# Computing v = x·wv by seven block products instead of eight, from batch 1 on, in a transformer block on one Trainium2 core

## The chip, the core and the metric

The kernel runs on one core of one Trainium2 chip. A core has five engines that run their own instruction streams and meet only at semaphores: TensorE (PE in the profile; its weight loads are listed as PEld), VectorE (DVE), ScalarE (ACT), GpSimd (POOL) and SyncE (SP), which here issues every DMA. TensorE writes its results into eight banks of PSUM, each 128 partitions by 512 float32 columns. The metric is device time in microseconds for one execution; lower is better.

## What is computed

The reference is one transformer block over 16 batches of 512 tokens of width 256 (8 heads of 128): a layer norm without scale, causal attention with rotary positions, and a feed-forward net with weights of +1 and -1, both added to the input.

```
xn = layernorm(x)                                # x: (16, 512, 256)
q, k, v = xn@wq, xn@wk, xn@wv                    # (b, h, 512, 128) each
q, k = rope(q), rope(k)
p = softmax(q@k.T / 128 - 1e30*(i < j))          # causal
attn = (p@v) @ wo
h = 2*relu(s0 * [xn, -xn]@(+-k0))                # 1024 wide
h = 2*relu(s1 * h@(+-k1))                        # 1024 x 1024
out = x + attn + s2 * h@(+-k2)
```

The change touches `xn@wv` in batches 1 to 15, how the partial sums of the 1024 x 1024 layer are held, and the order of everything.

## The kernel before, in words

**Precision by halves.** Each float32 operand is split into two float16 numbers, HI and LO (the rest), and a product is three matmuls: HI·HI, HI·LO, LO·HI. ACT makes a HI by a copy with a cast (`v_hi`, `o_hi`, `qk_hi`, `xp_hi`, `split_w_hi`), DVE or POOL makes the LO by a subtraction (`v_lo`, `o_lo`, `split_w_lo` on DVE, `qk_lo`, `xp_lo`, `h0t_lo` on POOL). The weights of +1 and -1 are exact in fp8, so products with them need two matmuls.

**x.** For batch b, SP loads x (`load_x`), DVE makes its statistics (`stats`), POOL normalises it (`normalise`) into the place in `XT` where its transpose will stand, ACT and POOL split it into `XP` (`xp_hi`, `xp_lo`), and SP's `turn_x` transposes XP by DMA into `XT`, from which all of the batch's first matmuls read. XT has two places, one for even and one for odd batches.

**v.** `v_proj(b, grp, t)` makes 128 tokens (tile t) of 4 heads (group grp) of v: 6 matmuls of 128 x 512, stationary operand from XT, moving operand 512 columns of wv. A batch has 8 of them, so 48 matmuls of 512 columns.

**Attention.** Per head and batch: `qk` (6 matmuls of 512 columns for q, 6 for k), rotation (`swap` on ACT, `crossed` on POOL, `straight` and `rotate` on DVE), `scores` into three banks, softmax (`row_max` on DVE, `exponent` on ACT, `inverse` on DVE, `p_hi`, `p_lo`), `turn_p` on SP (two DMA transposes of P), `values`, `o_hi`, `o_lo`, and for each half batch `project` with wo and `add_attn`, `send`.

**Feed-forward.** `layer0` makes h0 transposed. The 1024 x 1024 layer is made in blocks of 512 by a seven-product scheme already: DVE makes differences of h0's quarters (`difference`), POOL made the weights' sums once (`combine`), and `product(j, p, ...)` is product p of 7 for column half j, 16 matmuls of 256 columns. Products 1 and 6 build running sums in a bank; where a sum is needed twice, ACT copies the bank (`copy_sum`, three times for each j); product 5 is kept in SBUF (`keep_p5`) and added by DVE (`add_p5`). Then `h1_hi`, `h1_lo`, and `layer2`.

**Order.** Nothing is scheduled at run time. Each engine's stream is written out in the code: `sync_program`, `gpsimd_program`, `scalar_program`, `vector_program`, `tensor_program`. A call stands behind the `wait_ge` lines that it needs. Batches 4 to 14 are a loop (`for b in range(4, 15)`; on TensorE to 13), in which the names of the banks go by a table, `ROTATION`. An engine takes its instructions strictly in this order, so whatever stands behind a waiting instruction waits too. The first 60 us or so also hold the loading, scaling and splitting of the weights: `largest`, `power_of_two`, `powers`, `split_w_hi` and `split_w_lo` (12 of each: 4 for q, 4 for k, 2 for v, 2 for wo), `convert_k1`, `weight_block`, `combine`.

The helper `chain` records most of the simple matmuls, which is why q, k, v, layer 0 and wo all show as L238 in the profile. L699 is `product`, L683 `values`, L666 `scores`, L710 `layer2`.

## Time and profile before

| | |
|---|---|
| time, median of 3 runs | 1728.72 us (1728.67 to 1729.3) |
| the profiled execution: time, span | 1728.13 us, 1726.3 us |
| granted TensorE clock, mean | 0.999 |
| PE busy | 1713.5 us (99%), 12752 matmuls |
| PEld, DVE, ACT, POOL busy | 1202.2, 1386.2, 1467.6, 890.4 us (70%, 80%, 85%, 52%) |
| DMA | 134.08 MB moved, queues 40.1% of 16 engines' span |

Busy time is the time in which at least one instruction of the engine was under way. Matmuls are pipelined: the page's "mean ns of one" is from a matmul's start to the end of its drain (379 ns for 512 columns), while matmuls in a row start closer together than that; what a matmul costs is therefore read from long runs, a stretch of so many us divided by its count. The line "idle before, releaser" names the engine whose event ended most of the idle time before a group. An "issue" time is the engine's own sequencer. Windows give an engine's busy time in a stretch; in the steady part one batch is one period. A few records of matmuls can be missing from a trace, so counts are taken from the program.

### The profile page before, as it was taken

To read this page: it belongs to the slowest core of one execution; us is meant where nothing else is said; L and a number is where in the kernel's file an instruction comes from. 1 tells how busy PE (TensorE), PEld (TensorE's weight loads), DVE (VectorE), ACT (ScalarE), POOL (GpSimd) and SP (SyncE) were. 2 spreads that over 40 slices of the span, in tenths; PEclk is the share of its full clock that TensorE was granted. 3 is DMA by queue.
4 is the path that set the end of the run, shared out by engine and by line. 5 is a ranking of instruction groups with operands and counts; after the bars stand their busy time and mean duration, and the time that the engine had idled before them with its cause. 6 is when DMAs were issued, how large, how long until landed. Compare 5 with 4: busy or idle time off the path is not lost.

```text
span 1726.3 us, 34270 instructions
## 1 busy us (share of the span) xinstructions
PE 1713.5 (99%) x12752; PEld 1202.2 (70%) x12752; DVE 1386.2 (80%) x3374; ACT 1467.6 (85%) x3229; POOL 890.4 (52%) x696
## 2 busy tenths in 40 slices
PE   8999999999999999999999999999999999999999
PEld 4567667677676776767667676676767767677677
DVE  8997887887878878688787877878788787886875
ACT  7898897888979889798897988979789797897984
POOL 7654655354654635556354563555635556354531
PEclk9999999999999999999999999999999999999999
DMA  5234434343434433444434343344433534353343
GB/s 177 56 72 85 93 60 93 68 90 64 76 81 65 98 60 71 86 72 83 68 62 86 74 81 68 68 85 70 92 56 82 79 61 93 58 94 71 62 81 68
DMA packets 454838, 134.08 MB, mean 78 GB/s; under 512 B 434704, under 2 KB 453648, under 8 KB 454672
## 3 DMA queue, kind: packets, MB, share of 16 engines
q1 hardware_dynamic: 454672, 131.90, 40.1%
q8 instruction: 100, 1.64, 0.4%
q14 instruction: 66, 0.54, 0.1%
HBM read 14.94 MB, written 8.39 MB: 14 GB/s over the span
## 4 chain that ended last, share of the span: by engine, by line
PE 95%; ACT 2%; DVE 2%; DMA 1%; SPq 0%; issue 0%; POOL 0%; DVEq 0%; ACTq 0%
PE bank L238 44%; PE bank L699 21%; PE bank L683 12%; PE bank L666 12%; PE bank L710 6%; DMA v<-in_wk 1%; ACT bank L427 1%; DVE pt L514 0%; ACT ph L431 0%; DMA xnat<-in_x 0%; DVE hb L549 0%; DVE ph L585 0%; SPq L282 0%; DVE wq L537 0%; ACT tb L409 0%
## 5 line engine op out<-in xcount | busy, mean ns | idle before, releaser
L351 POOL TENSOR_TENSOR tb<-tb,sin 128x512 f32<-128x512 f32 x256 | 324.7, 1273 | 445.4 <-ACT tb L410 442.7
L354 POOL TENSOR_TENSOR qk<-tb,qk 128x512 f16<-128x512 f32 x256 | 295.7, 1160 | 284.3 <-ACT qk L413 284.1
L699 PE MATMUL bank<-hb,wa 128*128 128x256 f16 x3360 | 391.3, 273 | 0.2 <-DVE ph L585 0.2
L699 PEld LDWEIGHTS bank<-hb,wa 128*128 128x128 fp8e5 x3360 | 327.3, 98 | 53.7 <-DVE ph L585 0.4
L427 ACT ACTIVATE bank<-bank,nm,sc 128x512 f32<-128x512 f32 (+3 forms) x512 | 301.3, 591 | 2.6
L585 DVE SCALAR_TENSOR_TENSOR ph<-bank,rk,ph 128x512 f16<-128x512 f32 (+3 forms) x512 | 254.1, 545 | 23.0 <-ACT ph L431 21.3
L575 DVE CUSTOM_DVE_ANT_0 bank<-bank,mask 128x512 f32<-128x512 f32 (+3 forms) x512 | 238.5, 518 | 20.4 <-PE bank L666 20.1
L557 DVE TENSOR_TENSOR bank<-bank,cos 128x512 f32<-128x512 f32 x256 | 176.7, 697 | 87.3 <-ACT tb L410 87.1
L683 PEld LDWEIGHTS bank<-pt,v 128*128 128x128 f16 x2304 | 203.7, 98 | 41.5 <-DMA pt<-ph 0.8
L431 ACT ACTIVATE ph<-bank,rk 128x512 f16<-128x512 f32 (+3 forms) x512 | 230.1, 541 | 2.4 <-DVE rk L582 1.4
L683 PE MATMUL bank<-pt,v 128*128 128x256 f16 (+1 forms) x2304 | 231.1, 255 | 0.0
L666 PE MATMUL bank<-qk 128*128 128x512 f16 (+3 forms) x1536 | 229.6, 299 | 0.8 <-POOL qk L354 0.7
L413 ACT ACTIVATE qk<-tb 128x512 f16<-128x512 f32 x256 | 159.5, 635 | 48.9 <-PE bank L666 27.1
L666 PEld LDWEIGHTS bank<-qk 128*128 128x128 f16 x1536 | 133.6, 98 | 93.1 <-POOL qk L354 1.9
L561 DVE TENSOR_TENSOR tb<-bank,tb 128x512 f32<-128x512 f32 x256 | 175.0, 685 | 23.4 <-POOL tb L351 22.6
L238 PE MATMUL bank<-xT,wq 128*128 128x512 f16 x768 | 187.6, 381 | 3.2 <-DVE wq L537 3.2
L409 ACT ACTIVATE tb<-bank 64x512 f32<-64x512 f32 x256 | 151.9, 593 | 42.0 <-PE bank L238 33.8
L238 PE MATMUL bank<-wv,xT 128*128 128x512 f16 x768 | 185.2, 379 | 0.3 <-DVE ph L585 0.3
L238 PE MATMUL bank<-xT,wk 128*128 128x512 f16 x768 | 184.4, 379 | 0.0
L238 PE MATMUL bank<-wo,o 128*128 128x256 f16 x1536 | 172.9, 273 | 0.0
L238 PEld LDWEIGHTS bank<-wo,o 128*128 128x128 f16 x1536 | 150.1, 98 | 20.9
L358 POOL TENSOR_TENSOR hb<-rt,hb 128x1024 f16<-128x1024 f32 x60 | 127.8, 2130 | 55.7 <-ACT hb L443 55.7
(113 smaller groups left out, 2343.9 us busy)
## 6 DMA issues: line engine op xcount, KB each, us to landing
out<-xnat SPq DMA_DIRECT2D x32, 256.0 KB, 2.2
xnat<-in_x SPq DMA_DIRECT2D x15, 512.0 KB, 3.8
pt<-ph SPq DMA_TRANSPOSE x256, 4.3
o<-in_k SPq DMA_DIRECT2D x1, 1024.0 KB, 7.5
v<-in_wq SPq DMA_DIRECT2D x1, 1024.0 KB, 9.5
v<-in_wk SPq DMA_DIRECT2D x1, 1024.0 KB, 11.3
ph<-in_wv SPq DMA_DIRECT2D x1, 1024.0 KB, 13.5
o<-in_wo SPq DMA_DIRECT2D x1, 1024.0 KB, 10.9
```

Source lines behind the costliest of these rows:

```text
L238: m = pe.matmul(ps[:, cols[0]:cols[1]], l, r, start=start and n == 0, stop=signal is not None and n == last)
L351: pool.tensor_tensor(tb, tb, SIN[:], ALU.mult).then_inc(s_crossed, 1)
L354: pool.tensor_tensor(QK[:, g % 2, 2 * w + 1, :], TB[:, (2 * g + w) % TRING, :], QK[:, g % 2, 2 * w, :], ALU.subtract).then_inc(s_qk_lo, 1)
L427: act.activation(p, p, ACT.Exp, bias=NM[:, g % 4, i:i + 1], scale=SC[:, 0:1], accum_out=SM[:, g % 4, i:i + 1]).then_inc(s_exp, 1)
L431: act.activation(part(g, i, HI), tile_of(ps, i), ACT.Copy, scale=RK[:, g % 4, i:i + 1]).then_inc(s_P_hi, 1)
L557: dve.tensor_tensor(ps[:, :], ps[:, :], COS[:], ALU.mult).then_inc(s_straight, 1)
L561: dve.tensor_tensor(tb, ps[:, :], tb, ALU.add).then_inc(s_rot, 1)
L575: dve.tensor_tensor_reduce(out=s, in0=s, in1=MASK[:, 512 - WIDTH[i]:512], scale=1.0, scalar=-3.0e38, op0=ALU.add, op1=ALU.max, accum_out=M ...
L585: dve.scalar_tensor_tensor(part(g, i, LO), tile_of(ps, i), RK[:, g % 4, i:i + 1], part(g, i, HI), ALU.mult, ALU.subtract).then_inc(s_P_lo, 1)
L666: mm = pe.matmul(ps[:, col:col + w], l, m, start=i == tiles[0] and n == 0, stop=end)
L683: mm = pe.matmul(ps[:, 128 * i0:128 * i1], l, m, start=n == 1, stop=n == 18)
L699: mm = pe.matmul(ps[:, 256 * u:256 * u + 256], WA[:, w, k, (2 * j + u) * 128:(2 * j + u) * 128 + 128], HB[:, h, s, k, :], start=first and ...
```

## The change

Four things change.

1. **v by seven products.** In batches 1 to 15 the product x·wv is cut into 2 x 2 blocks (two token tiles by 128 of x's columns; 128 of wv's rows by 256 of its columns) and made by seven block products with running sums. `v_product(b, grp, p)` is 6 matmuls of 256 columns; a batch has 2 x 7. x's four sums are made by POOL from the normalised x (`x_sums`, 4 instructions), split (`tp_hi` on ACT, `tp_lo` on POOL) and transposed by a second DMA transpose (`turn_t`) into a new buffer `XS`, one for all batches. The running sums are copied by ACT (`copy_sum`, twice for each group), product 5 is kept in SBUF (`keep_v5`) and added by DVE (`add_v5`, twice for each group). The weights' four sums are made once by POOL (`v_weight_sum`), and eight blocks of wv are split instead of two larger ones. `v_hi` and `v_lo` write the same number of tiles as before.
2. **Batch 0** keeps eight products (`v_first`), with 12 matmuls of 256 columns for a tile instead of 6 of 512.
3. **Layer 1 with two copies** of running sums for each j instead of three; for one of the two sums that need product 5, DVE's addition writes into another bank (`add_p5_to`).
4. **All orders** are new, on all engines, the first batches and the last one included.

To make room, small buffers are merged (`RS` into `VE`, `RI` into `NM`, `RK` into `MX`, the identity and the scales into PT's start). XN of every batch now goes through XS: POOL's `normalise(b+1)` writes there and waits for batch b's last v product.

```diff
+V_PRODUCTS = {1: (0, 0, 0, 0), 2: (1, 0, 0, 1), 3: (6, 0, 2, 1), 4: (2, 1, 0, 1), 5: (3, 1, 0, 0), 6: (4, 1, 2, 1),
+              7: (5, 1, 2, 0)}
...
-        W = {n: sb("w" + n, [128, 2, 2048], F16) for n in "qkvo"}
+        W = {n: sb("w" + n, [128, 2, 2048], F16) for n in "qko"}
+        WV = sb("wv", [128, 7, 2, 512], F16)
...
+        XS = sb("xs", [128, 2, 4, 2, 128], F16)
...
+        def turn_t(sp, b):
+            sp.dma_start_transpose(XS[:].rearrange("p s t c n -> p (s t c) n"),
+                                   XP.rearrange("p s t m -> p (s t m)")).then_inc(s_xTT, 16)
...
+        def x_sums(pool, b):
...
+            pool.tensor_tensor(t1, b12, b11, ALU.subtract).then_inc(s_t1, 1)
+            pool.tensor_tensor(t3, b22, b12, ALU.subtract)
+            pool.wait_ge(s_t1, b)
+            pool.tensor_tensor(t2, b22, t1, ALU.subtract).then_inc(s_t2, 1)
+            pool.wait_ge(s_t2, b)
+            pool.tensor_tensor(t4, b21, t2, ALU.subtract).then_inc(s_tt, 1)
...
+        def keep_v5(act, ps):
+            act.activation(V5, ps[:, :], ACT.Copy).then_inc(s_v5, 1)
...
+        def add_v5(dve, ps, dst):
+            dve.tensor_tensor(dst[:, :], ps[:, :], V5, ALU.add).then_inc(s_vadd, 1)
...
+        def add_p5_to(dve, ps, dst):
+            dve.tensor_tensor(dst[:, :], ps[:, :], S5, ALU.add).then_inc(s_add, 1)
...
-        def v_proj(pe, b, grp, t, ps):
-            operands = []
-            for c in range(2):
-                operands += three(lambda s: XT[:, b % 2, s, t, c, :],
-                                  lambda s: W["v"][:, s, c * 1024 + grp * 512:c * 1024 + grp * 512 + 512])
-            chain(pe, ps, (0, 512), operands, s_v)
...
+        def v_product(pe, b, grp, p, ps):
+            w, buffer, t, c = V_PRODUCTS[p]
+            src = XS if buffer else XT[:, b % 2]
+            for u in range(2):
+                operands = three(lambda s: src[:, s, t + u, c, :], lambda s: WV[:, w, s, grp * 256:grp * 256 + 256])
+                for n, (l, r) in enumerate(operands):
+                    end = u == 1 and n == 2
+                    mm = pe.matmul(ps[:, 256 * u:256 * u + 256], l, r, start=p in (1, 5) and u == n == 0, stop=end,
+                                   skip_group_check=True)
...
         ROTATION = [
-            [0, 5, 1, 3, 4, 2, 6, 7],
+            [2, 0, 1, 7, 4, 5, 3, 6],
...
```

**TensorE, middle of a batch.** In rows before, inside batch 7, the v products are eight lots of 6 matmuls of 512 columns (`bank<-wv,xT 128x512`), and the first matmul that needs the next batch's x (the wait for s_xT) stands behind all products of layer 1 (L699) but one:

```order
L699 MATMUL bank1<-hb,wa 128x256 x16
L238 MATMUL bank0<-wv,xT 128x512 [waits s_h1]
L238 MATMUL bank0<-wv,xT 128x512 x5
L683 MATMUL bank3<-pt,v 128x256 [waits s_P_lo,s_pt1]
...
L238 MATMUL bank6<-xT,wq 128x512 [waits s_xT,s_P_lo]
L238 MATMUL bank6<-xT,wq 128x512 x5
```

In rows of the changed kernel, in the same batch (its names of lines: L803 `product`, L276 `chain`, L754 `scores`, L792 `v_product`), the wait for s_xT stands in the middle of layer 1, and the v products that wait for the transposed sums (s_xTT) and for copies (s_copy) follow, in lots of 6 matmuls of 256 columns:

```order
L803 MATMUL bank5<-hb,wa 128x256 x16
L276 MATMUL bank6<-xT,wq 128x512 [waits s_xT,s_o]
L276 MATMUL bank6<-xT,wq 128x512 x5
L276 MATMUL bank4<-xT,wq 128x512 [waits s_h1]
...
L792 MATMUL bank1<-wv,xT 128x256 [waits s_copy]
L792 MATMUL bank1<-wv,xT 128x256 x5
L792 MATMUL bank4<-wv,xs 128x256 [waits s_xTT]
L792 MATMUL bank4<-wv,xs 128x256 x5
```

What moved: the next batch's x is now needed with four products of layer 1 still to come, where it was needed with one to come, and the lots of v are narrower and wait for more.

**SP, one batch.** Before, x's transpose (`xT<-rt`) is followed at once by the transposes of P:

```order
L252 DMA xnat<-in_x 128x4x256 [waits s_out01,s_out00]
L282 DMA_TRANSPOSE pt<-ph 128x16x128 [waits s_PV,s_P_lo]
L282 DMA_TRANSPOSE pt<-ph 128x8x128
L282 DMA_TRANSPOSE pt<-ph 128x16x128 [waits s_PV]
L282 DMA_TRANSPOSE pt<-ph 128x8x128
L276 DMA_TRANSPOSE xT<-rt 128x16x128 [waits s_xp]
L282 DMA_TRANSPOSE pt<-ph 128x16x128 [waits s_PV,s_P_lo]
```

In the changed kernel a second transpose stands between them, for the sums (`xs<-rt`), with a wait of its own:

```order
L290 DMA xnat<-in_x 128x4x256 [waits s_out01,s_out00]
L324 DMA_TRANSPOSE pt<-ph 128x16x128 [waits s_PV]
L324 DMA_TRANSPOSE pt<-ph 128x8x128
L324 DMA_TRANSPOSE pt<-ph 128x16x128 [waits s_PV,s_P_lo]
L324 DMA_TRANSPOSE pt<-ph 128x8x128
L314 DMA_TRANSPOSE xT<-rt 128x16x128 [waits s_xp]
L318 DMA_TRANSPOSE xs<-rt 128x16x128 [waits s_tp]
L324 DMA_TRANSPOSE pt<-ph 128x16x128 [waits s_PV,s_P_lo]
```

What moved: the next P's transposes now also wait for s_tp.

**TensorE, the start.** Before, layer 0 of batch 0 (`xT,w0`) begins when the first quarter of its weights is signed, and one lot waits for h0's bank; layer 1 (`hb`) begins on the first of h0:

```order
L238 MATMUL bank2<-xT,w0 128x512 [waits s_xT0,s_W0]
L238 MATMUL bank2<-xT,w0 128x512
L238 MATMUL bank2<-xT,w0 128x512 [waits s_xT0]
...
L238 MATMUL bank2<-xT,w0 128x512 [waits s_h0]
L238 MATMUL bank2<-xT,w0 128x512 x3
L238 MATMUL bank3<-hb 128x512 [waits s_h0,s_W1]
...
L238 MATMUL bank4<-dg,pt 128x2
```

In the changed kernel the last lot of layer 0 stands behind the scale's power (`128x2`, waits s_pow), and layer 1's third step waits for the last of h0:

```order
L276 MATMUL bank1<-pt 128x128 [waits s_largest]
L276 MATMUL bank4<-pt 128x2 [waits s_ones,s_pow]
L276 MATMUL bank3<-xT,w0 128x512 x4
L276 MATMUL bank2<-hb 128x512 [waits s_W1]
L276 MATMUL bank2<-hb 128x512 x3
L276 MATMUL bank2<-hb 128x512 [waits s_W1]
L276 MATMUL bank2<-hb 128x512
L276 MATMUL bank2<-hb 128x512 [waits s_h0]
```

On ACT the step that makes that last of h0 from bank 3 (`hb<-bank3`) stands behind five copies of layer 1's weights (`wa`, L443) and one split of wq (L465); before, all eight such steps stood ahead of them:

```order
L468 ACTIVATE hb<-bank6 128x512
L443 ACTIVATE wa<-rt 128x1024 [waits s_W1a]
L443 ACTIVATE wa<-hb 128x1024 [waits s_W1]
L443 ACTIVATE wa<-hb 128x1024 [waits s_W1a]
L443 ACTIVATE wa<-hb 128x1024
L443 ACTIVATE wa<-rt 128x1024
L465 ACTIVATE wq<-v,kn 128x2x256 [waits s_w_in_q,s_KN]
L468 ACTIVATE hb<-bank3 128x512 [waits s_l0]
```

What moved: one eighth of h0 is made later, and layer 1 of batch 0 waits for it.

## Rows read from the trace of the kernel before

**Rows 1.** Page: busy time of the engines.
```profile
PE 1713.5 (99%) x12752; PEld 1202.2 (70%) x12752; DVE 1386.2 (80%) x3374; ACT 1467.6 (85%) x3229; POOL 890.4 (52%) x696
```
**Rows 2.** Windows, one period: length, busy PE, PEld, DVE, ACT, POOL, clock, DMA.
```profile
460.35:566.46 106.11, 106.11 (x802) 75.27 (x800) 85.17 (x210) 91.00 (x202) 54.73 (x43) 1.00 0.43 75
```
**Rows 3.** Chain of waits in time: start, length, what, count.
```profile
294.05 5.24 PE bank L699 x48
430.93 3.88 PE bank L238 x18
1674.50 1.63 PE bank L666 x12
1717.37 1.65 PE bank L683 x18
```
**Rows 4.** Groups by line and form: busy us, mean ns of one, idle before.
```profile
L238 PEld LDWEIGHTS bank<-wv,xT 128*128 128x128 f16 x768 | 74.4, 98 | 70.1 <-DVE ph L585 0.8
L446 ACT ACTIVATE bank<-bank 128x512 f32<-128x512 f32 x90 | 53.5, 594 | 22.4 <-PE bank L699 21.4 <-DVE h L605 1.0
L405 ACT ACTIVATE rt<-xT 128x1024 f16<-128x1024 f32 x15 | 15.9, 1063 | 0.0
L602 DVE TENSOR_TENSOR bank<-bank,rt 128x512 f32<-128x512 f32 x60 | 41.7, 695 | 12.9 <-PE bank L699 10.7 <-ACT bank L446 1.0
L351 POOL TENSOR_TENSOR tb<-tb,sin 128x512 f32<-128x512 f32 x256 | 324.7, 1273 | 445.4 <-ACT tb L410 442.7
L347 POOL TENSOR_TENSOR rt<-xT,rt 128x1024 f16<-128x1024 f32 x15 | 31.9, 2128 | 2.9 <-ACT rt L405 2.9
L537 DVE SCALAR_TENSOR_TENSOR wv<-ph,kn,wv 128x1024 f16<-128x1024 f32 x2 | 2.7, 1368 | 0.0
```
**Rows 5.** Timeline of PE at the start: start, length, instruction, idle before.
```profile
31.38 1.89 PE L238 MATMUL bank<-xT,wq 128*128 128x512 f16 x4 [3.20 <-DVE wq L537]
```
**Rows 6.** Timeline of ACT at the start.
```profile
22.02 3.00 ACT L378 ACTIVATE wa<-hb 128x1024 fp8e5<-128x1024 f16 x3
26.28 1.38 ACT L396 ACTIVATE wq<-v,kn 128x512 f16<-128x512 f32 x2
```
**Rows 7.** Timeline of DVE: the last of the reductions, and splits of weights.
```profile
25.80 2.27 DVE L514 TENSOR_REDUCE pt<-o 128x1 f32<-128x2048 f32 x1
62.27 1.32 DVE L537 SCALAR_TENSOR_TENSOR wo<-o,kn,wo 128x1024 f16<-128x1024 f32 x1
68.45 3.15 DVE L537 SCALAR_TENSOR_TENSOR wo<-o,kn,wo 128x1024 f16<-128x1024 f32 x1
```
**Rows 8.** Timeline of POOL beside the last of these.
```profile
68.39 2.12 POOL L347 TENSOR_TENSOR rt<-xT,rt 128x1024 f16<-128x1024 f32 x1 [2.92 <-ACT rt L405]
```
**Rows 9.** Windows at the start, columns as in rows 2.
```profile
20.00:40.00 20.00, 16.04 (x68) 6.97 (x67) 19.79 (x30) 17.53 (x26) 18.42 (x10) 0.91 0.20 64
40.00:60.00 20.00, 19.68 (x102) 9.58 (x101) 19.59 (x49) 17.22 (x32) 17.49 (x21) 1.00 0.01 2
```
**Rows 10.** Timeline of one batch: PE's step behind `project`, x's transpose, its first use.
```profile
1011.82 1.46 PE L238 MATMUL bank<-xT,wk 128*128 128x512 f16 x6
1034.71 1.92 SPq L276 DMA_TRANSPOSE xT<-rt  x1
1056.87 1.46 PE L238 MATMUL bank<-xT,wq 128*128 128x512 f16 x6
```
**Rows 11.** Line L282 (`turn_p`), all of them: from issue to landing.
```profile
DMA to landing us min/median/max: 3.1/4.3/6.1
```
**Rows 12.** Line L276 (`turn_x`), all of them: from issue to landing.
```profile
DMA to landing us min/median/max: 4.2/4.2/4.6
```
**Rows 13.** Timeline of SP: the last pair of `turn_p`.
```profile
1709.79 3.72 SPq L282 DMA_TRANSPOSE pt<-ph  x2
```
**Rows 14.** Windows behind it, columns as in rows 2 (last: DMA's share, GB/s).
```profile
1711.00:1712.00 1.00, 1.00 (x12) 0.90 (x10) 0.00 (x0) 0.00 (x0) 0.00 (x0) 1.00 1.08 209
1714.00:1715.00 1.00, 1.00 (x11) 0.90 (x10) 0.46 (x1) 0.51 (x1) 0.00 (x0) 1.00 0.80 148
```

More of the change, by code:

```diff
@@ L809, in sync_program @@
             turn_p(sp, 11)
-            sp.wait_ge(s_xp, 2)
-            turn_x(sp, 2)
+            sp.wait_ge(s_tp, 2)
+            turn_t(sp, 2)
             sp.wait_ge(s_P_lo, 52)
@@ new lines, in tensor_program @@
+            pe.wait_ge(s_rot, 19)
+            values(pe, 7, BANK[7])
+            v_product(pe, 1, 1, 7, BANK[1])
+            pe.wait_ge(s_rot, 20)
+            product(pe, 0, 1, range(8), BANK[4], first=True)
+            pe.wait_ge(s_vadd, 4)
+            v_product(pe, 1, 1, 4, BANK[1])
+            pe.wait_ge(s_qk_lo, 18)
+            scores(pe, 8, 0, BANK[6])
+            pe.wait_ge(s_rot, 21)
+            scores(pe, 8, 1, BANK[0])
+            pe.wait_ge(s_vp, 15)
+            scores(pe, 8, 2, BANK[3])
@@ new lines, in tensor_program @@
+            pe.wait_ge(s_P_lo, 80)
+            values(pe, 16, BANK[1])
+            pe.wait_ge(s_h1, 9)
+            product(pe, 1, 1, range(8), BANK[3], first=True)
+            pe.wait_ge(s_copy, 14)
+            product(pe, 0, 7, range(8), BANK[4])
+            product(pe, 0, 3, range(8), BANK[2])
+            pe.wait_ge(s_pt[1], 288)
+            pe.wait_ge(s_rot, 44)
+            values(pe, 17, BANK[7])
+            pe.wait_ge(s_qk_lo, 43)
+            pe.wait_ge(s_rot, 45)
+            scores(pe, 20, 0, BANK[0])
@@ L6065, in tensor_program @@
+            scores(pe, 114, 2, BANK[5])
             pe.wait_ge(s_sum, 27)
@@ new lines, in tensor_program @@
+            values(pe, 112, BANK[1])
+            pe.wait_ge(s_h1, 105)
+            product(pe, 1, 1, range(8), BANK[3], first=True)
+            pe.wait_ge(s_copy, 110)
+            product(pe, 0, 7, range(8), BANK[4])
+            product(pe, 0, 3, range(8), BANK[2])
+            pe.wait_ge(s_pt[1], 1824)
+            pe.wait_ge(s_rot, 236)
+            values(pe, 113, BANK[7])
+            pe.wait_ge(s_qk_lo, 235)
+            pe.wait_ge(s_rot, 237)
+            scores(pe, 116, 0, BANK[0])
```

8750 lines of the change are left out of this document (4813 added, 3937 removed), and 26 rows, old and new, of the table ROTATION.

## The prediction

> **What bounds the kernel now.** The first view is the page's line of busy times: TensorE is busy 1713.5 of 1726.3 us, ScalarE 85%, VectorE 80%, GpSimd 52% [rows 1]. A busy share says nothing yet, so the second view is a window of exactly one batch: in 106.11 us TensorE is busy 106.11, ScalarE 91.00, VectorE 85.17, GpSimd 54.73, at a granted clock of 1.00 [rows 2]. There is no idle time on TensorE to take away in the middle; only fewer or shorter matmuls help, and whatever makes TensorE wait costs in full. The third view, the chain of waits, gives what a matmul costs in a row: 48 matmuls of 256 columns take 5.24 us, 109.2 ns each; 18 of 512 columns take 3.88 us, 215.6 ns each [rows 3]. The fourth is the start, where TensorE does wait: 3.20 us for the first weights of q [rows 5], while VectorE is busy 39.4 us of the 40 from 20 to 60 us [rows 9]. So two places matter: a batch's matmuls, fifteen times, and the start, once, where VectorE is the full engine.
>
> **The sum of the matmuls.** Per batch v takes 8 x 6 = 48 matmuls of 512 columns: 48 x 215.6 ns = 10.35 us. By seven products it takes 2 x 7 x 6 = 84 of 256 columns: 84 x 109.2 ns = 9.17 us [rows 3]. The gain is 1.18 us a batch, 17.7 us over batches 1 to 15. It is a little under one part in eight of v, since 2 x 109.2 - 215.6 = 2.8 ns of each matmul don't shrink with its width. Batch 0's eight products become 96 of 256 columns: 96 x 109.2 = 10.48 us, 0.13 us more. No other matmul is added or taken away, so TensorE's work falls by 17.6 us. All the rest of the change can only take from this.
>
> **Weight loads.** Each matmul here loads its own stationary operand, 98 ns [rows 4], and a product's 109.2 ns leaves 11 ns beside it. Products of layer 1 already run in this form, one load for each 256 columns, and their pace is the one used above; so I charge the loads nothing. The Trainium skill (TensorE: Matmul & The Clock Gate, section Back-to-back issue gap) says that in a real stream of loads and matmuls the pace is set by both, and gives 131 ns for 512 columns and 81 ns for 128. By it, with an estimate of 98 ns for 256 columns on the line between the page's two, v would go from 6.3 to 8.2 us a batch, and the change would cost 28 us where the rows give 17.6 back. The trace here contradicts the pace of 131 ns.
>
> **Work added to the other engines, per batch.** ScalarE: two more copies in all (four for v, two fewer for layer 1) and two `keep_v5`, each like L446's 594 ns, and `tp_hi`, like `xp_hi`'s 1063 ns: 3.4 us, so 94.4 us of a period of 104.9 us, 90%. VectorE: four `add_v5` like L602's 695 ns: 2.8 us, so 88.0 us, 84%. GpSimd: `tp_lo` like L347's 2128 ns, and four additions of 256 elements; these have no row, and lie between 532 ns (a quarter of L347's) and 1273 ns (L351, twice their size) [rows 4]. I take 0.85 us, on the line through the two: 5.5 us, so 60 us, 57%. All three stay under TensorE, so by amount they cost nothing. What they can cost is lateness: an engine at 90% in a fixed order serves a request late more often. The nearest rows are two periods of before without any wait at 91.00 of 106.11; the bounds are nothing and, say, two copies' length a batch. I take nothing, and leave the rest to the rivals.
>
> **Copies.** A copy of a running sum now stands close behind its product: `v_product(b,1,1)` is followed by one head's scores, 1.63 us [rows 3], and then `v_product(b,1,6)` waits for the copy, 0.594 us [rows 4]. About 1 us is left over. Between product 6 and product 3, which also waits for a copy, stand two products of 0.66 us; 0.7 us is left. In before the closest such pair had a q or k product and one of layer 1 between, 3 us. If ScalarE is in the middle of something else, each of these places waits for up to one instruction of its queue.
>
> **x's transpose.** Counted from the end of `project(b-1, 1)`, TensorE reached the first use of the next batch's x after 45.05 us (1056.87 - 1011.82), and the transpose was issued after 22.9 us, so with 4.2 us to land it had some 18 us to spare [rows 10, 12]. Now five q or k lots (1.295 us each, a third of 3.88), nine products of layer 1 (1.747 each, a third of 5.24), two `values` (1.65) and one head's scores (1.63) stand between [rows 3]: 6.5 + 15.7 + 3.3 + 1.6 = 27.1 us. SP's queue puts the transpose behind two pairs of `turn_p`, and the second pair waits for `values(8b+1)`, which ends after four of these lots, six products and two `values`: 19.0 us. A pair takes SP 3.72 us [rows 13] and its transfers last to 5.0 us behind its start (from 1709.79 to 1714.80, the last window being busy for 0.80 us) [rows 14]. x's own 2048 columns, 0.52 MB at the 209 GB/s of that view, take 2.5 us behind them. So xT lands at 19.0 + 5.0 + 2.5 = 26.5 us against a need at 27.1. It is just in time, and I charge nothing; the upper bound comes from the slowest landing of `turn_p`, 6.1 against a median of 4.3 us [rows 11]: 1.2 us of waiting a batch, or 1.8 if my count of the margin is off by its 0.6. Behind `turn_x` now stands `turn_t`, which waits for `tp_lo`, and behind that the next P's transposes. The sums are through at about 35 us (`xp_lo` at 20.5, four additions, the rotations between, `tp_hi`, `tp_lo`), and the `values` that needs that P comes at 47 us, so this wait is covered.
>
> **The start.** Now one eighth of h0 is made late: on ScalarE it stands behind five copies of about 1.0 us (3.00 us for three) and a split of q, which puts it at 28.1 us where before q's splits began at 26.28 [rows 6]. VectorE's reduction of wo ends at 28.1 anyway [rows 7], so h0 is complete at 28.8. Then come 10 matmuls of one lot of layer 1 and 16 of the next, 26 x 215.6 ns = 5.6 us, and q's first lot starts at 34.4 us instead of 31.38 [rows 5]. That is 3.0 us. Before, that lot began at the low clock of 1.2 GHz (four matmuls in 1.89 us, 0.91 granted over the window [rows 5, 9]), after 3.20 us of waiting; if it begins at 2.4 GHz now, 1.3 us come back. I take 2.4 us of 1.7 to 3.0. Further, VectorE splits eight lots of 512 elements for v where it split two of 1024 in 2.7 us [rows 4]. A lot of 1024 took 1.32 us, and 3.15 us when GpSimd ran a two-input operation beside it [rows 7, 8]: so 2.6 to 9.9 us more. VectorE has no room before 60 us, but four of the eight can come later, and are ordered so. I take 1.6 us, near the low end, of 0 to 9.9. The start costs 4.0 us together.
>
> **The end.** The last head's `values` began at 1717.37 and its P had landed at 1714.80: 2.6 us to spare [rows 3, 14]. Between its scores and that `values` stood 60 matmuls with wo, both halves of `layer2` and one `values` (6.6 + 7.0 + 1.6 = 15.2 us at 109.2 ns a matmul of 256 columns); now one `values` more and one half of `layer2` less, 13.3 us. 0.7 us are left: nothing.
>
> **The sum.** 1728.13 us of the profiled execution (its span of 1726.3 us and 1.8 around it) - 17.6 + 4.0 = 1714.5 us; the median of the runs lies 0.6 us above it: 1715.1. I forecast 1715 us.
>
> **The rivals.**
> 1. Copies served late. For: ScalarE at 90%, and 0.7 to 1 us of room at two places a batch. Against: nothing in the steady part of before waited at 86%. One copy's length, 0.6 us, a batch at 14 batches: + 8.3, 1723 us.
> 2. VectorE bounds the start. For: 39.4 of 40 us busy. Against: half the new splits are put off. The upper end of 9.9 instead of 1.6 us: 1723 us.
> 3. xT comes late (the other side). Place: the first q lot of the next batch, batches 2 to 15. For: a margin of 0.6 us by my count, two pairs of transposes ahead of it on one queue, landings up to 6.1 us [rows 11]. Against: x's own landings were all within 4.2 to 4.6 [rows 12]. With 1.3 us a batch, 14 x 1.3 = + 18.2: 1733 us. It decides from 1.0 us a batch on, where the gain is gone.
> 4. The start is no worse than before: TensorE's order makes up the late eighth of h0. 1711 us.
> 5. Weight loads are not hidden: 98 + 107 ns for each narrow matmul, 84 x 205 ns = 17.2 us a batch, + 6.9 x 15: some 1830 us. Against: L699's pace. The Trainium skill's page on TensorE, cited above, speaks for this one, with a smaller price.
>
> **Chances.** Forecast (1712 to 1719 us) 0.57; rival 1, 0.15; rival 2, 0.08; rival 3, 0.11; rival 4, 0.08; rival 5, 0.01. Range: below, rival 4 and 2 us of its own uncertainty, 1709; above, to the middle of rival 3 between no wait and 1.3 us, 1729. Within 0.2% (3.5 us, what a measurement of this kernel can tell from no change) is 1725.3 to 1732.2. Rivals 1, 2 and 4 and the forecast are faster but for their upper tails; rival 3 is split between same and slower. Faster 0.82, same 0.09, slower 0.09.
>
> **What would show it.** In a window of one batch: a period of 104.9 us, TensorE busy all of it, ScalarE 94.4, VectorE 88.0, GpSimd 60. Narrow v matmuls at 109 ns in the chain. TensorE's waits: none by name in the middle; a wait on the DMA of xT repeated 14 times would be rival 3, one on ScalarE's copy in a bank rival 1. At the start the first matmul with wq at 34.4 us and TensorE's idle time up to 60 us some 3 to 4 us more than before. The prediction is wrong if the period is over 106 us, or if TensorE is idle over 25 us in all.

## The result, and the profile after

| | before | after |
|---|---|---|
| time, median (4 runs each) | 1728.7 us (1728.59 to 1729.3) | 1745.33 us (1743.47 to 1747.16) |
| profiled execution: time, span | 1728.13, 1726.3 us | 1747.16, 1745.4 us |

The change makes the kernel slower: ratio 1.0095, 95% interval 1.0078 to 1.0113. The forecast was 1715 us with a range of 1709 to 1729; the result lies outside it, 30 us above the forecast, and on the other side of the kernel before. The page's line of busy times, which answers to [rows 1]:

```profile
PE 1706.3 (98%) x13340; PEld 1258.5 (72%) x13340; DVE 1425.0 (82%) x3440; ACT 1514.8 (87%) x3310; POOL 968.1 (55%) x775
```

TensorE is busy 7.2 us less, in a span 19.1 us longer: its idle time is 39.1 us where it was 12.8. Who ended it is in the view of waits (engine, line, who was waited for, us in total, times, longest):

```profile
PE bank L771 <- DMA pt<-ph: 7.8, 10, 1.4
PE bank L276 <- DMA xT<-rt: 5.8, 11, 1.2
PE bank L276 <- DVE pt L606: 4.8, 1, 4.8
PE bank L276 <- ACT w L435: 3.0, 1, 3.0
PE bank L754 <- DVE tb L639: 2.6, 1, 2.6
PE bank L754 <- POOL qk L419: 2.4, 3, 1.6
...
PE bank L276 <- DVE tb L639: 1.6, 1, 1.6
```

The first two are of the steady part, about once a batch each (one of the ten waits for P is at the very end), the next two of the start, and the others shown of batches 0 to 2. Windows of the changed kernel say how much each stretch holds (columns as in rows 2), and the last two rows show the start, whose clock was 1.00 and 0.91:

```profile
60.00:300.00 240.00, 229.40 (x1740) 162.32 (x1739) 207.89 (x514) 218.03 (x488) 140.65 (x116) 1.00 0.41 78
300.00:1670.00 1370.00, 1357.48 (x10788) 1013.51 (x10786) 1121.33 (x2736) 1206.49 (x2650) 767.67 (x606) 1.00 0.44 80
...
0.00:20.00 20.00, 13.89 (x54) 9.57 (x55) 12.58 (x28) 10.02 (x14) 11.39 (x19) 0.75 0.93 320
20.00:40.00 20.00, 15.24 (x60) 6.64 (x58) 17.84 (x20) 16.54 (x23) 18.23 (x11) 0.82 0.19 61
```

The same two long windows of the kernel before, which were not shown above:

```profile
60.00:300.00 240.00, 239.09 (x1736) 161.79 (x1734) 199.55 (x489) 213.77 (x483) 134.49 (x104) 1.00 0.43 82
300.00:1670.00 1370.00, 1369.95 (x10317) 969.95 (x10316) 1100.53 (x2704) 1177.30 (x2606) 700.04 (x537) 1.00 0.41 75
```

So from 300 us on TensorE waits 12.5 us where it waited 0.05, between 60 and 300 us 10.6 where it waited 0.9, at the end once for 1.4, and up to 60 us 2.3 us more: 25.9 us together. Two things come on top, both estimates from rows. In front of a wait the last matmul's drain counts as busy, while in a row of matmuls the next one starts before it is over (273 - 109 ns, or 379 - 216): 0.165 us for each of 26 more waits (36 against 10), 4.3 us. And the low clock at the start, below, costs some 4 us more than before. Against that stands what the seven products save, 16.4 us: 1.10 us a batch (below) in 15 batches, less the 0.13 us of batch 0. 25.9 + 4.3 + 4 - 16.4 = 17.8 us, of the span's 19.1.

**One batch.** A window over eleven batches, from one start of `project` to the same eleven batches later:

```profile
378.07:1546.74 1168.67, 1158.43 (x9199) 864.53 (x9197) 957.83 (x2343) 1031.67 (x2267) 655.22 (x517) 1.00 0.44 80
```

That is a period of 106.24 us, where 104.9 was forecast and 106.11 was before, with 0.93 us idle in each. In batch 6 the transposes on SyncE, first the row of both pairs of P's, then the second pair by itself, x's and the sums' transposes, and, from the chain, the time from x's issue to its landing. Then TensorE's lot behind `project`, and its first lot with the next batch's x:

```profile
726.27 10.64 SPq L324 DMA_TRANSPOSE pt<-ph  x4
733.20 3.71 SPq L324 DMA_TRANSPOSE pt<-ph  x2
736.96 3.29 SPq L314 DMA_TRANSPOSE xT<-rt  x1
749.95 1.97 SPq L318 DMA_TRANSPOSE xs<-rt  x1
736.96 5.42 DMA xT<-rt
```
```profile
714.01 1.46 PE L276 MATMUL bank<-xT,wq 128*128 128x512 f16 x6
742.51 2.75 PE L276 MATMUL bank<-xT,wq 128*128 128x512 f16 x12 [1.22 <-DMA xT<-rt]
```

And one batch on, `values` of the fifth head (h = 4), and before it the issue of its P's transpose:

```profile
862.50 1.91 SPq L324 DMA_TRANSPOSE pt<-ph  x1
```
```profile
860.62 3.55 PE L771 MATMUL bank<-pt,v 128*128 128x256 f16 x36
864.00 0.82 PE L792 MATMUL bank<-wv,xT 128*128 128x256 f16 x6
864.66 0.82 PE L792 MATMUL bank<-wv,xs 128*128 128x256 f16 x6
865.31 1.79 PE L754 MATMUL bank<-qk 128*128 128x512 f16 x12
866.94 1.47 PE L792 MATMUL bank<-wv,xs 128*128 128x256 f16 x12
869.72 1.82 PE L771 MATMUL bank<-pt,v 128*128 128x256 f16 x18 [1.31 <-DMA pt<-ph]
```

The row x36 is two heads' `values`, 2 and 3. P has two places (`s_pt[0]` and `s_pt[1]`), so head 4's transpose waits until head 2's `values` has read the first, at 860.62 + 1.65 = 862.27 us; it is issued at 862.50. P itself had been complete since 850.0 us, when VectorE's last `p_lo` of that head ended, so only the place was missing. Between the two `values` stand 5.9 us of matmuls, and from the first issue to the second landing the pair takes 7.2 us here (to 869.68). In the trace of the kernel before, no two `values` that share a place stood closer than 10.5 us (10.6 us in batch 7, from 805.75 to 816.36), and no pair took longer than 7.3 us. The wait for the sums' transpose (xs, issued 855.45) has nothing to do with it.

**The start.** TensorE's rows that answer to [rows 5]:

```profile
14.32 9.15 PE L276 MATMUL bank<-xT,w 128*128 128x512 f16 x28 [3.04 <-ACT w L435]
23.31 0.38 PE L276 MATMUL bank<-pt 128*128 128x128 f32 x2
28.45 0.59 PE L276 MATMUL bank<-pt 128*128 128x2 f32 x2 [4.76 <-DVE pt L606]
28.90 1.87 PE L276 MATMUL bank<-xT,w 128*128 128x512 f16 x4
30.56 4.43 PE L276 MATMUL bank<-hb 128*128 128x512 f16 x12
...
39.15 1.46 PE L276 MATMUL bank<-xT,wq 128*128 128x512 f16 x6
```

Layer 0 begins at 14.32 us (before: 12.02), since its first lot needs the last of four signs of k0. Its 28 matmuls take 9.15 us where 28 x 215.6 ns are 6.0: the granted clock is 1.2 GHz for half of these 20 us (0.75 in the window above), and it had fallen already in the window from 10 to 11 us (0.53), ahead of the wait for the signs. Then TensorE waits 4.76 us for the power of two, which stands on VectorE behind the maximum of wv, and in that wait, between 27 and 28 us, the clock falls a second time (0.56). The first lot with wq comes at 39.15 us, not at 34.4.

### The profile page after: what moved, and what is told of

The parts are those of the page before. It is cut to its first block, busy times and chain, and to the rows that moved or that the text cites. A ratio compares the mean times of both kernels' runs of the same rounds, so it can differ in the third digit from the quotient of the medians.

```text
span 1745.4 us, 35757 instructions
## 1 busy us (share of the span) xinstructions
PE 1706.3 (98%) x13340; PEld 1258.5 (72%) x13340; DVE 1425.0 (82%) x3440; ACT 1514.8 (87%) x3310; POOL 968.1 (55%) x775
## 4 chain that ended last, share of the span: by engine, by line
PE 79%; ACT 6%; DMA 6%; DVE 4%; SPq 3%; issue 1%; POOL 1%; DVEq 0%; ACTq 0%
PE bank L276 32%; PE bank L803 16%; PE bank L771 10%; PE bank L754 9%; PE bank L792 6%; PE bank L814 5%; SPq L324 3%; DMA xT<-rt 3%; DMA pt<-ph 3%; ACT bank L505 2%; DVE ph L670 1%; POOL tb L416 1%; ACT tb L485 1%; ACT tb L484 1%; DVE bank L660 1%
## 5 line engine op out<-in xcount | busy, mean ns | idle before, releaser
L803 PE MATMUL bank<-hb,wa 128*128 128x256 f16 x3360 | 388.2, 273 | 0.0
L803 PEld LDWEIGHTS bank<-hb,wa 128*128 128x128 fp8e5 x3360 | 328.1, 98 | 49.9
L505 ACT ACTIVATE bank<-bank,nm,sc 128x384 f32<-128x384 f32 (+3 forms) x512 | 302.8, 595 | 2.7
L670 DVE SCALAR_TENSOR_TENSOR ph<-bank,mx,ph 128x512 f16<-128x512 f32 (+3 forms) x512 | 254.1, 543 | 12.7 <-ACT ph L509 11.8
L660 DVE CUSTOM_DVE_ANT_0 bank<-bank,mask 128x128 f32<-128x128 f32 (+3 forms) x512 | 238.0, 512 | 2.6 <-PE bank L754 2.0
L509 ACT ACTIVATE ph<-bank,mx 128x512 f16<-128x512 f32 (+3 forms) x512 | 231.0, 537 | 5.3 <-DVE mx L667 3.6
L754 PE MATMUL bank<-qk 128*128 128x512 f16 (+3 forms) x1536 | 230.1, 299 | 5.1 <-DVE tb L639 2.6
L754 PEld LDWEIGHTS bank<-qk 128*128 128x128 f16 x1536 | 132.4, 98 | 91.4 <-POOL qk L419 3.8
L276 PE MATMUL bank<-xT,wq 128*128 128x512 f16 x768 | 184.7, 379 | 7.5 <-DMA xT<-rt 5.8
L276 PE MATMUL bank<-xT,wk 128*128 128x512 f16 x768 | 184.1, 379 | 1.3 <-DVE v L645 0.9
L484 ACT ACTIVATE tb<-bank 64x512 f32<-64x512 f32 x256 | 151.9, 593 | 26.5 <-PE bank L276 20.2
L276 PE MATMUL bank<-wo,o 128*128 128x256 f16 x1536 | 172.9, 273 | 0.0
L276 PEld LDWEIGHTS bank<-wo,o 128*128 128x128 f16 x1536 | 150.3, 98 | 20.3
L485 ACT ACTIVATE tb<-bank 64x512 f32<-64x512 f32 x256 | 150.6, 588 | 3.1
```

What stands on the lines that cost most here:

```text
L276: m = pe.matmul(ps[:, cols[0]:cols[1]], l, r, start=start and n == 0, stop=signal is not None and n == last)
L505: act.activation(p, p, ACT.Exp, bias=NM[:, g % 4, i:i + 1], scale=SC[:, 0:1], accum_out=SM[:, g % 4, i:i + 1]).then_inc(s_exp, 1)
L509: act.activation(part(g, i, HI), tile_of(ps, i), ACT.Copy, scale=RK[:, g % 4, i:i + 1]).then_inc(s_P_hi, 1)
L660: dve.tensor_tensor_reduce(out=s, in0=s, in1=MASK[:, 512 - WIDTH[i]:512], scale=1.0, scalar=-3.0e38, op0=ALU.add, op1=ALU.max, accum_out=M ...
L670: dve.scalar_tensor_tensor(part(g, i, LO), tile_of(ps, i), RK[:, g % 4, i:i + 1], part(g, i, HI), ALU.mult, ALU.subtract).then_inc(s_P_lo, 1)
L754: mm = pe.matmul(ps[:, col:col + w], l, m, start=i == tiles[0] and n == 0, stop=end)
```

## Experiments

Each was timed beside the kernel before on the same chip. Given are the median, the ratio to the kernel before with its 95% interval, and mostly the difference to the changed kernel's 1745.3 us. The kernel before took 1728.6 to 1729.0 us in the different groups of runs, so a difference between runs of two groups carries up to 0.4 us more doubt than its medians show.

### SyncE: x's transpose ahead of the second pair of P's

```diff
+                sp.wait_ge(s_xp, b + 1)
+                turn_x(sp, b + 1)
                 sp.wait_ge(s_P_lo, 32 * b + 16)
                 sp.wait_ge(s_PV, 8 * b + 2)
                 turn_p(sp, 8 * b + 3)
                 sp.wait_ge(s_xp, b + 1)
-                turn_x(sp, b + 1)
```

> SyncE's order alone: from batch 3 on the next batch's x is transposed ahead of the second pair of P's transposes instead of behind it. Theory A (two tight places in one batch, xT at the first q lot and P of the fifth head at its values, that cover for each other: what one lets through the other takes): the 11 waits on xT (5.8 us idle) go, those on P of the fifth head grow; 1742 us, 1740 to 1745. Theory B (the two places are independent): 1745.3 - 7.6 = 1738 us. Theory C (another engine, ScalarE at 90 per cent, sets the period of 106.2 us, and the waits only show it): 1745 us, no change.

Measured: 1738.52 us, 1.0057 (1.0044 to 1.0069), 6.8 us less. No wait on xT is left; those on P hardly change:

```profile
PE bank L771 <- DMA pt<-ph: 7.2, 8, 1.5
```

Theory B's 7.6 us is nearly there; A's 3 us and C's nothing are refuted.

### TensorE: the fifth head's values 2.4 us later

```diff
                 v_product(pe, b + 1, 0, 7, ps[5])
+                pe.wait_ge(s_vp, 8 * b + 9)
+                v_product(pe, b + 1, 0, 3, ps[4])
+                product(pe, 1, 4, range(8), ps[2])
                 pe.wait_ge(s_pt[0], 128 * b + 96)
                 pe.wait_ge(s_vp, 8 * b + 9)
                 values(pe, 8 * b + 4, ps[1])
-                v_product(pe, b + 1, 0, 3, ps[4])
-                product(pe, 1, 4, range(8), ps[2])
```

> TensorE's order alone: the values of each batch's fifth head stand behind the next v product and product 4 of layer 1's second half (2.4 us later) from batch 2 to 13. Theory A: the waits on P of the fifth head go, those on xT grow from 0.2 to 1.2 us a batch; 1742 us, 1739 to 1745. Theory B (independent places): 1745.3 - 5.5 = 1740 us. Theory C: 1745 us.

Measured: 1741.37 us, 1.007 (1.0056 to 1.0083), 4.0 us less. The waits on P fall from 7.8 to 3.1 us and those on xT grow by a tenth:

```profile
PE bank L276 <- DMA xT<-rt: 6.4, 12, 1.3
PE bank L771 <- DMA pt<-ph: 3.1, 4, 1.4
```

### Both

> Both of the two edits before together. Theory A: neither wait is left, the period falls from 106.24 to the 104.9 us of its matmuls over 12 batches, 1745.3 - 15 = 1730 us, 1729 to 1733. Theory B: 1745.3 - 7.6 - 5.5 = 1732 us, so this run alone does not tell A from B, but with the two single ones it does. Theory C: the waits move to ScalarE or VectorE and the time stays over 1740 us.

Measured: 1733.06 us, 1.0023 (1.0013 to 1.0033), 12.3 us less; the two alone make 10.8. The places are nearly independent (B); theory A, that what one lets through the other takes, is wrong. P still makes TensorE wait 3.6 us, at five places. And the period is what the matmuls make of it; a window from one `project` to the next:

```profile
903.71:1008.72 105.01, 105.01 (x839) 78.78 (x837) 86.94 (x213) 93.78 (x208) 59.61 (x47) 1.00 0.44 81
```

TensorE is busy all of 105.01 us, 1.10 us less than the 106.11 of [rows 2]. ScalarE at 93.78, VectorE at 86.94 and GpSimd at 59.61 are where the prediction put them (94.4, 88.0, 60), and none makes TensorE wait. What two reorderings repair is what the new order had broken.

### The price of a product, with the order repaired

The run all_warm, on which this one rests, is the last of the start's kernels below.

```diff
                 operands = three(lambda s: src[:, s, t + u, c, :], ...)
+                if p == 7:
+                    operands = operands + operands
                 for n, (l, r) in enumerate(operands):
-                    end = u == 1 and n == 2
+                    end = u == 1 and n == len(operands) - 1
```

> The kernel of the run all_warm, in which the last of the seven products of v runs its six matmuls twice (v is not the reference's then), so that TensorE has as many narrow matmuls for v as eight products would take: 12 more of 256 columns a batch, 180 in all. Theory A (with the two places repaired TensorE alone bounds the period, and a product left out is worth its matmuls): 180 x 109.2 ns = 19.7 us more, 1747 us, 1746 to 1748. Theory B (ScalarE or VectorE nearly bound the period too): under 16 us more, 1740 to 1743 us.

Measured: 1744.5 us, 1.0094 (1.008 to 1.0107), 17.2 us above all_warm. One batch is 106.33 us, TensorE busy throughout:

```profile
800.62:906.95 106.33, 106.33 (x850) 79.94 (x849) 87.05 (x214) 94.01 (x207) 59.59 (x47) 1.00 0.41 80
```

That is 1.32 us more than the 105.01 us above, for 12 matmuls, 110 ns each, load and all: theory A in every batch, 19.7 us in 15. The total is 2.5 us less than that and lies between the ranges given for A (1746 to 1748 us) and B (1740 to 1743). TensorE is idle 23.1 us in this run and 25.5 in all_warm; the waits for P in batch 14 (0.5 us) and at the very end (1.5 us) are gone.

### The order of k0's signs alone

ScalarE signs, and VectorE subtracts, block 0 first and block 3 last, and TensorE's first lot waits for one instead of four:

```diff
-            pe.wait_ge(s_W0, 4)
+            pe.wait_ge(s_W0, 1)
             pe.wait_ge(s_xT0, 1)
             layer0(pe, 0, 1, 0, BANK[2])
```

> The changed kernel with nothing but the order of the four signs of k0 changed, so that TensorE's first lot of layer 0 needs the first of them and not the last. It begins at 12.3 instead of 14.3 us. Theory A (what bounds the start behind it is VectorE's power of two, 27.3 to 28.4 us, behind its maximum of wv): nothing comes of it, 1745 us, at most 1 us less. Theory B (TensorE's late start and low clock bound the start): 1745.3 - 2 to 3 = 1742.5 to 1743 us.

Measured: 1744.28 us, 1.0088 (1.0074 to 1.0102), 1.0 us less, which theory A allows; a difference of that size is within the spread of both kernels' runs. Layer 0 starts at 12.38 us, 1.9 us sooner, and TensorE then waits longer for the power of two:

```profile
12.38 8.12 PE L276 MATMUL bank<-xT,w 128*128 128x512 f16 x28 [0.69 <-DVE xT L588]
20.34 0.38 PE L276 MATMUL bank<-pt 128*128 128x128 f32 x2
25.78 0.59 PE L276 MATMUL bank<-pt 128*128 128x2 f32 x2 [5.05 <-DVE pt L606]
```

### The start: signs, power of two and the last eighth of h0

Beside the signs, in excerpts:

```diff
             largest_of_all(dve, 0, BANK[1])
-            dve.wait_ge(s_w_in["v"], 16)
-            largest(dve, 2)
+            dve.wait_ge(s_am_max, 1)
+            power_of_two(dve, 0)
...
             h0_first_hi(act, 4, BANK[6])
+            act.wait_ge(s_l0, 8)
+            h0_first_hi(act, 3, BANK[3])
...
+            layer1(pe, 0, range(2, 3), BANK[2])
             pe.wait_ge(s_pow, 1)
             pe.wait_ge(s_ones, 1)
             spread_power(pe, 0, BANK[4])
```

> The start alone: the block of k0 that TensorE's first lot of layer 0 needs is subtracted and signed first instead of last, so TensorE starts at 12.1 instead of 14.3 us; VectorE makes the power of two right behind the maximum of all, and its maximum of wv later; the last eighth of h0 is made ahead of the five copies of layer 1's weights; the small matmuls that spread the power stand behind layer 1's first three steps. Theory A (the start's loss is made there): first wq matmul at 32 to 34 us instead of 39.15, 17 us of half clock shrink to 3 to 7, and the time is 1745.3 - 6 = 1739 us, 1737 to 1741. Theory B (VectorE is the full engine of the start; what TensorE gains before 40 us it waits away at its first scores and between 60 and 140 us): 1743 to 1745 us.

Measured: 1741.96 us, 1.0074 (1.0062 to 1.0087), 3.4 us less, between the ranges of the two theories. The first lot of wq comes at 33.49 us, 5.7 us sooner, after 2.5 us of waiting for wq's split on VectorE. At the low clock (0.91 from 20 to 40 us) its six matmuls take 2.23 us instead of 1.46, and 3.9 us of the 5.7 are left from 60 us on. All waits behind stand where they stood, 3.9 us earlier and as long as before (2.63, 0.40, 1.05, 0.93 us): what is gained here is not waited away there.

### Everything so far together

With two small edits more: `v_product(1, 0, 6)` behind `qk(7, 0)`, and the last head's P on VectorE ahead of `add_ffn(15, 0)`.

> The start's edits and the two of the steady part together, and two small ones: in batch 1 the v product that waited for ScalarE's copy of a running sum (1.02 us at 124 us) stands behind one q lot more, and at the end VectorE makes the last head's P ahead of an addition of the feed-forward net that stood before it. Theory A (the losses stand at separate places and add up): 1733.1 - 3.4 (start) - 1.2 (copy) - 0.7 (end) = 1728 us, 1726 to 1730. Theory B (something gained at the start is waited away later, since VectorE and ScalarE are full up to 140 us): 1730 to 1733 us.

Measured: 1728.54 us, 1.0001 (0.9992 to 1.001): theory A. The losses were at separate places and add up; the kernel is where it was before the change. The two small edits moved waits more than they removed them: the wait for the copy in batch 1 (1.02 us) is gone, but 0.92 us is waited one lot later, and P at the end still comes 1.5 us late.

### Dummy products at the start

```diff
             turn_first(pe, 0, BANK[0], BANK[1])
+            zeros(pe, 1, BANK[7])
...
-            zeros(pe, 2, BANK[7])
+            zeros(pe, 5, BANK[7])
```

> The kernel of the run before with five more dummy products of zeros in TensorE's first 12 us (one behind each of the first two transposes of x, three more in front of layer 0), which fill its idle time there. Theory A (the idle time before 12 us is why the granted clock falls to 1.2 GHz at about 10 us): the clock stays at 2.4 GHz up to the wait for wq, layer 0's seven lots take 6 instead of 8.6 us, TensorE then waits for other engines for part of it; 1 to 2 us less than the run before. Theory B (the clock falls there whatever TensorE does, or the time gained is waited away at the first of wq): the same time within 0.5 us, or up to 0.5 us more from the dummy products.

Measured: 1727.27 us, 0.9991 (0.9982 to 1.0000), 1.3 us below the run before: theory A in kind. The granted clock is 1.00 over the first 20 us (0.91 in all_fixed, where layer 0's 28 matmuls took 7.99 us), and 26 matmuls of layer 0 take 5.79 us:

```profile
13.39 5.79 PE L276 MATMUL bank<-xT,w 128*128 128x512 f16 x26 [0.41 <-DVE xT L588]
```

This is the best version that computes the reference. Against the kernel before it is not a difference that can be told from none. The saving is in it all the same: TensorE is busy 1700.0 us, 13.5 less than before, and idle 25.5 us, 12.7 more. Of that idle time 9.6 us more stand between 60 and 300 us, 1.8 us more between 300 and 1670, and 1.5 us at the end.

### VectorE's splits of wv cut short

In the kernel of all_fixed, `split_w_lo` for v makes 64 columns of each group of 256 (GpSimd zeroes the low halves once).

> The kernel of the run before the last with VectorE's eight splits of wv's blocks cut to an eighth of their width and no more (64 of 512 columns; the rest of wv's low halves is zero, so v is less exact): VectorE has some 6 us less work up to 100 us. Theory A (VectorE's added splits bound TensorE between 60 and 240 us): the waits at 65 to 135 us (2.6, 0.4, 0.9, 0.3, 0.6 us) go in the main, 3 to 5 us less than with whole splits. Theory B (these waits come from ScalarE's chain and the order of single instructions): 0 to 1.5 us less.

Two groups of 64 are a quarter of 512, not the eighth that the expectation says: the eight splits take 5.0 us instead of 9.4. Measured: 1727.97 us, 0.9994 (0.9985 to 1.0003), 0.6 us below all_fixed. That is theory B, and not more than the runs' spread. The wait at 64 us is 2.63 us instead of 2.81, and those at 125 to 133 us are as long as they were (0.9, 0.7, 0.3, 0.6). Half of the splits stand in front of the first, all of them in front of the others: with 4.4 us less work on VectorE, its splits are not their cause.

### Single instructions earlier in batches 0 and 1

```diff
             straight(dve, BANK[7])
+            dve.wait_ge(s_crossed, 6)
+            dve.wait_ge(s_straight, 6)
+            rotate(dve, 2, 1, BANK[7])
+            dve.wait_ge(s_x[1], 16)
+            stats(dve, 1)
             dve.wait_ge(s_S, 4)
             row_max(dve, 1, 3, BANK[1])
...
+            rotate(dve, 14, 0, BANK[4])
             dve.wait_ge(s_S, 41)
             row_max(dve, 13, 2, BANK[2])
...
+            qk_hi(act, 14, 0)
             act.wait_ge(s_inv, 13)
             act.wait_ge(s_pt[0], 192)
             p_hi(act, 12, 3, BANK[5])
```

The same calls are taken out further down, and on GpSimd `crossed(2, 1)` stands ahead of `combine(6, 0)`.

> The kernel of the run all_warm with four single instructions moved in batches 0 and 1: VectorE rotates the third head's k ahead of x's statistics and of two row maxima, GpSimd makes its crossed part ahead of a sum of layer 1's weights; VectorE rotates the q of head 14 ahead of a row maximum, and ScalarE makes its high half ahead of four pieces of P. Theory A (the waits of batches 0 to 2 are single instructions too late in a fixed order): the 2.8 us wait at 64 us shrinks to 1.5 or less, those of 1.6 and 1.7 us at 213 and 217 us to 1.5 together; 1727.3 - 2.5 = 1725 us. Theory B (ScalarE and VectorE are full there, so that what is made earlier makes something else later): the sum of the waits between 60 and 240 us stays within 1 us of its 9.5 us, 1727 us.

Measured: 1730.87 us, 1.001 (1.0001 to 1.0019), 3.6 us above all_warm: worse than either theory. Of all_warm, then of this run, TensorE at 64 us:

```profile
63.72 0.50 PE L754 MATMUL bank<-qk 128*128 128x256 f16 x3 [2.81 <-DVE tb L639]
64.62 1.47 PE L276 MATMUL bank<-xT,wk 128*128 128x512 f16 x6 [0.41 <-DVE ph L670]
```
```profile
66.45 2.27 PE L276 MATMUL bank<-xT,wk 128*128 128x512 f16 x6 [3.96 <-DVE ph L670]
```

The wait for the rotation is gone, but the next lot needs P, which VectorE makes later now: 2.81 + 0.41 became 3.96 us in one piece. Behind it six matmuls of 512 columns take 2.27 instead of 1.47 us, at a lower granted clock: in the window of 60 to 80 us it is 0.91, where all_warm has 1.00. The same happens at 223 us (1.58 + 1.65 + 0.85 became 0.44 + 1.54 + 1.93 us, clock 0.91 from 220 to 240). TensorE is idle 10.8 us between 60 and 240 us, against 10.5 (B). The two stretches at 1.2 GHz cost more than that: 0.91 over 20 us is some 3.5 us of it, and up to half of that is lost, twice. The profiled execution is 4.7 us above all_warm's, and 1.3 us of this stand already at 60 us, ahead of the moved instructions: the clock was low on the first lots with wq (2.74 us for the first six matmuls, 1.47 in all_warm), as it was in eighth_product, whose start has the very order of all_warm. The medians can't tell how often that happens.

### Less work for ScalarE, VectorE, or both, in batches 1 and 2

In the kernel of all_warm, in batches 1 and 2, so that v is not the reference's there: `act.activation(dst[:, 0:64], src[:, 0:64], ACT.Copy)` for v's copies and a narrow `tp_hi`; `dve.tensor_tensor(dst[:, 0:64], ps[:, 0:64], V5[:, 0:64], ALU.add)` for `add_v5`; in the third run both, and `keep_v5` narrow.

> The kernel of the run all_warm with less work for ScalarE in batches 1 and 2 alone: the eight copies of v's running sums there are 64 instead of 512 columns wide, and the two first high halves of x's sums 32 instead of 256 wide (v of these batches is not the reference's). That is 8 x 0.4 + 2 x 0.75 = some 4.7 us less of ScalarE between 75 and 235 us. Theory A (ScalarE, full there with 19.7 of 20 us, makes TensorE wait): the waits between 120 and 240 us (6.5 us idle) fall by 3 us or more, 1724 us. Theory B (VectorE, or the order): under 1 us less, 1726.5 to 1727.5 us.

> The kernel of the run all_warm with less work for VectorE in batches 1 and 2 alone: the eight additions of product 5 are 64 instead of 512 columns wide (v is not the reference's there), some 8 x 0.45 = 3.6 us less. Theory A (ScalarE makes TensorE wait): under 1 us less. Theory C (VectorE does, with 19.3 to 19.8 of 20 us between 80 and 120 us): the waits between 120 and 240 us fall by 2 us or more, 1725 us.

> Both cuts at once, and the four copies of product 5 in batches 1 and 2 cut to 64 columns too (v is not the reference's there). Theory A: as cut_scalar and 0.5 us more, 1723 to 1724 us. Theory C: as cut_vector. If the two engines release the waits only together, this run is over 2 us below both others. If all three stay within 1 us of 1727.3 us, the added work of v in these batches is not what TensorE waits for there, but the order of the whole.

Measured: 1726.61 us, 0.9983 (0.9974 to 0.9991); 1727.79 us, 0.9995 (0.9986 to 1.0004); 1725.79 us, 0.9982 (0.9973 to 0.9991). That is 0.7 us less, 0.5 more and 1.5 less than all_warm, timed on another chip; 0.5 and 0.7 us are of the size of the doubt, 1.5 us is over it. The first is what theory B expected (under 1 us), the second rules out theory C, VectorE's 2 us or more; the third is half of theory A's 3 to 4 us, and above the 1 us that was to mean that the amount of work has no part. TensorE's busy time from 60 to 300 us, of all_warm and of cut_both:

```profile
60.00:300.00 240.00, 229.54 (x1754) 163.44 (x1752) 205.71 (x504) 216.98 (x485) 142.40 (x112) 1.00 0.43 80
```
```profile
60.00:300.00 240.00, 231.09 (x1776) 165.64 (x1775) 203.56 (x506) 213.75 (x486) 143.02 (x114) 1.00 0.44 81
```

Of 10.5 us idle 1.6 go with the added work of both engines. 8.9 us stay, at the same places, 2.8 and 0.4 us at 64 us and 1.6, 1.4 and 0.85 us at 212 to 219 us. So most of it is not the amount of v's added work. What is left is how the new order lays the whole of batches 0 to 2, each q, k and P in a chain over three engines. Which part of that order, no run here shows; the four instructions that I moved did not mend it.

## Why the prediction was wrong

**Where the time is.** The profiled execution took 1747.16 us where the sum of the prediction gave 1714.5. The gap of 32.6 us is, with 0.165 us of drain for each wait and so an estimate: the waits for xT and P in the steady part, 15.5 us; batches 0 to 2, 11.0; the start, 3.8 beyond the 4.0 that were forecast; the end, 1.6; the matmuls, 1.2.

**The step that failed in the steady part: the margins of the transposes.** The prediction put xT's landing at 26.5 us behind `project` against a need at 27.1, called that just in time and charged nothing. In batch 6 `project` ends at 714.01, the second pair is issued at 733.20 (19.2 us, forecast 19.0), x's transpose at 736.96, and it lands at 742.4 us: 28.4. Over the batches it is 27.3 to 28.4. The chain in front was right to 0.2 us. What was wrong is the end: 5.0 us for the pair and 2.5 for x's columns, 7.5 together, taken from a view of how long transfers last. In the runs x's transpose is issued 3.5 to 4.5 us after the pair's first (3.76 in most batches) and lands 4.3 to 5.4 us after its own issue (median 4.4): 8.1 to 9.2 us. The rows at hand, 3.72 us [rows 13] and 4.2 us [rows 12], would have given 7.9, a landing at 26.9 us and 0.2 us to spare, so they alone would not have shown a wait. The failed step is to call a margin of 0.6 us enough and to charge nothing, when the rows named a spread of 0.4 us for x's landings and of 3 us for P's on the same queue. Why some of x's landings now take 4.7 to 5.4 us, where 4.6 was the longest before, no run isolates. It also is the mechanism of rival 3, given 0.11 at 1.3 us a batch; it measured 5.8 us idle in 11 batches, 6.8 us of time.

**The wait that was not looked for: P of the fifth head.** The prediction asked whether the new wait for the sums holds P back, and was right that it does not. It did not ask how far apart `values(g)` and `values(g + 2)` stand, which share a place of P. The new order leaves 5.9 us between those of heads 2 and 4, where 10.5 us was the shortest distance before; where TensorE waited, issue to landing of the pair took 6.4 to 7.2. Standing later, these `values` gave back 4.0 us alone and 5.5 us together with the other edit, with no term and no rival in the prediction.

**Both came from one habit.** The sum took TensorE's work of before and after, and charged the moved order nothing except where I had looked. Before, the steady part waited 0.05 us in 1370; the new order was taken to be as tight.

**The matmuls.** The forecast was 17.7 us over 15 batches; the clean period shows 1.10 instead of 1.18 us a batch, 16.5. The step was right, 7% too large. The weight loads stay hidden: 110 ns for a load and 256 columns. The Trainium skill (TensorE: Matmul & The Clock Gate, section Back-to-back issue gap), with an estimate of 98 ns between its two figures, would put them 12 ns lower; the measurement decides.

**The start.** The forecast was + 4.0 us. By the lots of wq it is 7.8 us late (39.15 against 31.38). The late eighth of h0, which carried the forecast, is not what TensorE waited for: the power of two was later (4.76 us), the signs cost 2.3, and the clock was low twice: 28 + 12 + 4 matmuls took 15.4 us where 10.0 are due. The second fall came within the wait for the power of two. The first came before the wait for the signs, and with the signs in order it was still there (28 matmuls in 8.12 us); only the dummy products took it away. Reordering the start brought 3.4 us, the dummy products 1.3. The splits on VectorE were charged 1.6; they grew by 6.7 us (9.4 against 2.7 [rows 4]), inside their bounds, but cutting 4.4 us of it away brought 0.6.

**Batches 0 to 2.** The prediction had no term for them, and TensorE has 9.7 us of idle time more there than before, the largest loss that stayed open: neither the amount of work nor the four moved instructions explain it. The prediction's count of the steady part began at batch 1 as if the order were the same there. Rival 1, copies served late, appeared once (1.02 us, batch 1); in the steady part the busy ScalarE made TensorE wait nowhere, as costed.

**The end.** It was charged nothing, with 0.7 us to spare; P of the last head is 1.40 us late. The landing at 1714.80 us was read from the DMA's share of the last window. By the landings in the same trace the pair was there at 1715.30, 5.5 us after its issue, and none of the 128 pairs took less; here the last pair took 6.75.

**The forecast's own alarms** were right: a period over 106 us and over 25 us idle.

## What to carry to other kernels

Where a change redraws an order, walk every resource with few places (here P's two, x's one transpose queue) through one batch of the new order, issue by issue, and take each landing from the row of its own kind; a margin under 1 us is a charge, not a cover. Put the slack's sign in the sum: a new order in a kernel without idle time has 15 chances to lose a microsecond and none to win one. Here two such places cost 12.3 us of a forecast gain of 13.6. Reckon first batches and start apart, and count a long wait of TensorE at more than its length where the granted clock falls behind it.
